# Expert tiles of a two-layer decoder: a counted loop with four places, or straight code with six

## The reference

```python
logits = flat @ router_w.T                      # 2048 tokens, 16 experts
_, topk_idx = jax.lax.top_k(logits + router_bias, 2)
# combine[n, e]: the share of expert e in token n, two non-zero entries a token
for e in range(16):
    h = jax.nn.silu(flat @ Wu[e]) * (flat @ Wg[e])      # 512 -> 256
    out = out + combine[:, e:e + 1] * (h @ Wd[e])       # 256 -> 512
# and one shared expert of twice the width
```

## Time and profile before

| | us |
|---|---|
| median of 3 runs | 2899.99 |
| lowest and highest | 2896.42, 2900.81 |
| the profiled execution's own time | 2895.5 |
| its span, first to last instruction | 2893.8 |

### The profile page before, as it was taken

How to read it: one execution, slowest core, us unless ns; L and a number is a source line. 1 busy time by engine, 2 the same in 40 slices (tenths; PEclk the granted TensorE clock), 3 DMA queues, 4 the chain that set the end, 5 groups by cost and what they waited for, 6 DMA issues and landing times. The chain is left out here.

```text
span 2893.8 us, 34373 instructions
## 1 busy us (share of the span) xinstructions
PE 2060.3 (71%) x12276; PEld 1397.2 (48%) x12308; DVE 1880.0 (65%) x3042; ACT 1168.0 (40%) x2024; POOL 777.1 (27%) x616
## 2 busy tenths in 40 slices
PE   5999995578787848888569999952002688677760
PEld 5777774122222214555357777730002677555540
DVE  3456555467786746999735566547887333688876
ACT  2323222385665634454223232216872112465540
POOL 1212223005969101110012122210000040566654
PEclk7999997598998879999769999987555589999995
DMA  4432231662425020000033332300001100799965
GB/s 138 96 67 60 52 67 45 165 199 80 134 83 147 29 91 0 1 1 1 0 109 67 67 67 45 67 17 0 0 0 45 60 1 0 256 308 303 309 225 166
DMA packets 83672, 258.06 MB, mean 89 GB/s; under 512 B 17312, under 2 KB 18848, under 8 KB 73424
## 3 DMA queue, kind: packets, MB, share of 16 engines
q0 software_dynamic: 29856, 153.33, 17.6%
q1 hardware_dynamic: 52656, 102.62, 12.9%
q10 hardware_dynamic: 1024, 0.26, 0.0%
HBM read 167.51 MB, written 37.79 MB: 71 GB/s over the span
## 5 line engine op out<-in xcount | busy, mean ns | idle before, releaser
L875 DVE TENSOR_REDUCE x_negm<-x_M 128x2 f32<-128x1024 f32 x256 | 309.2, 1223 | 110.5 <-PE x_M L935 110.0
L824 ACT ACTIVATE x_PT<-x_T 128x512 f32<-128x512 f32 x512 | 280.1, 598 | 199.5 <-PE x_T L955 194.2
L317 ACT ACTIVATE L_attn_PT<-L_attn_T 128x512 f32<-128x512 f32 x320 | 175.4, 595 | 360.5 <-PE L_attn_T L519 360.5
L387 DVE TENSOR_REDUCE L_attn_negm<-L_attn_M 128x2 f32<-128x1024 f32 (+1 forms) x192 | 192.0, 1041 | 59.0 <-PE L_attn_M L500 58.5
L224 POOL DMA_DIRECT2D L_attn_QKS<-L_attn_HL x64 | 34.7, 543 | 600.5 <-ACT L_attn_HL L302 566.7
L955 PE MATMUL x_T<-x_QS,x_KS 49*128 49x512 f32 x512 | 141.2, 548 | 62.9 <-ACT x_PT L824 42.6
L517 PE MATMUL L_attn_T<-L_attn_QKS 97*128 97x256 f32 (+3 forms) x512 | 164.8, 384 | 11.7 <-DMA L_attn_QKS<-L_attn_mT 9.4
L1400 PE MATMUL graph_P<-ident,graph_L 128*128 128x128 f32 x64 | 15.7, 428 | 214.8 <-DVE graph_L L1473 209.5
L964 PE MATMUL x_O<-x_PT,x_V 128*32 128x512 f32 x1024 | 156.2, 686 | 7.1 <-issue 7.1
L1421 ACT ACTIVATE graph_seen_a<-graph_SIM,graph_mid 128x512 bf16<-128x512 f32 x200 | 141.4, 708 | 34.3 <-DVE graph_mid L1453 34.3
L955 PEld LDWEIGHTS x_T<-x_QS,x_KS 49*128 49x128 f32 x512 | 52.2, 201 | 210.7 <-ACT x_PT L824 135.1
(11 more groups left out here) (369 smaller groups left out, 5638.2 us busy)
## 6 DMA issues: line engine op xcount, KB each, us to landing
L_attn_QKS<-L_attn_HL SPq DMA_DIRECT2D x192, 128.0 KB, 4.7
L_attn_QKS<-L_attn_HL POOLq DMA_DIRECT2D x192, 128.0 KB, 4.1
moe_y_rows<-slots_YS SPq DMA_DIRECT2D x48, 256.0 KB, 7.8
x_WRAW<-in_w_gateT POOLq DMA_DIRECT2D x8, 1024.0 KB, 7.2
x_QS<-x_xh SPq DMA_DIRECT2D x128, 64.0 KB, 2.3
x_WRAW<-in_w_upT POOLq DMA_DIRECT2D x8, 1024.0 KB, 5.3
x_WRAW<-in_w_downT POOLq DMA_DIRECT2D x8, 1024.0 KB, 6.0
ffn_w<-x_WTER POOLq DMA_DIRECT2D x12, 512.0 KB, 3.2
```

Source lines behind the costliest of these rows:

```text
L317: ac.activation(PT[:, s, bank], T[:, bank], ACT.Exp, scale=SCALE).then_inc(t_free, 1)
L387: last = ve.tensor_reduce(negm[:, g % 2, h0:h0 + nh, i], src, AX.X, ALU.max, negate=True)
L824: ac.activation(PT[:, s // 4, head(s), :], T[(STEPS_S * g + s) % 3][:], ACT.Exp, scale=SCALE).then_inc(t_free, 1)
L875: ve.tensor_reduce(negm[:, g % 2, u // 4:4:2, u % 4], m[:].rearrange("p (r k) -> p r k", r=2), AX.X, ALU.max, negate=True).then_inc(m_free, 1)
```

## The change

`SLOT_TILES` becomes 47. The sum of ceil(c / 128) over 16 experts with 4096 pairs is at most 47. In `run_slots` the counted loops go: each engine's program is written out for all tiles. RAW and XG have six places, YS four, PICK is gone, and the indirect DMAs read their columns from the tables. GpSimd only issues fetches; VectorE makes all the low parts of the weights, the second up piece as one more instruction between HL and XTL. ScalarE in place of VectorE copies Y to YS, two tiles behind, between HH and XTH. TensorE's order is the same, but its first eight products of U wait for `up_hi`, and the last four for `up_lo`.

```diff
-    SLOT_TILES = 2 * NTILE + NE
+    SLOT_TILES = 2 * NTILE + NE - 1
...
-    RING = 4
-    TURNS = SLOT_TILES // RING
+    RING, LAST = 6, SLOT_TILES - 1
...
-        YS = places("YS", RING, D, F32)
-        PICK = places("PICK", RING, 2, U32)
+        YS = places("YS", 4, D, F32)
...
         @block.gpsimd
         def _(pool):
+            for t in range(SLOT_TILES):
+                n = t % RING
+                if t >= RING:
+                    pool.wait_ge(down_lo, t - RING + 1)
+                    pool.wait_ge(up_lo, 2 * (t - RING + 1))
+                pool.indirect_dma_start(out=XG[n], out_offset=None, in_=T["x_rows"],
+                                        in_offset=bass.IndirectOffsetOnAxis(T["slot_token"][:, t:t + 1], 0)
+                                        ).then_inc(x_in[n], 16)
+                pool.indirect_dma_start(out=RAW[n], out_offset=None, in_=weights,
+                                        in_offset=bass.IndirectOffsetOnAxis(T["weight_row"][:, t:t + 1], 0)
+                                        ).then_inc(w_in[n], 16)
...
         @block.scalar
+            def take_y(t):
+                act.wait_ge(y_full, t + 1)
+                if t >= 4:
+                    act.wait_ge(y_out[t % 4], 16 * (t // 4))
+                ac.activation(YS[t % 4], Y[t % 2][:], ACT.Copy).then_inc(y_taken, 1)
+
+            up_weights(0)
+            turned(0)
+            for t in range(SLOT_TILES + 2):
+                if t < LAST:
+                    up_weights(t + 1)
+                if 1 <= t <= SLOT_TILES:
+                    act.wait_ge(ht_full, t)
+                    ac.activation(HH[:], HT[:, 0:F], ACT.Copy).then_inc(h_hi, 1)
+                if t >= 2:
+                    take_y(t - 2)
+                if t < LAST:
+                    turned(t + 1)
+                if t <= LAST:
+                    act.wait_ge(u_full, t + 1)
+                    ac.activation(SU[t % 2], U[t % 2][:, 0:F], ACT.Silu).then_inc(silu_done, 1)
+                    if t >= 2:
+                        act.wait_ge(y_full, t - 1)
+                    ac.activation(WH[t % 2][:, DOWN], RAW[t % RING][:, DOWN], ACT.Copy).then_inc(down_hi, 1)
...
         @block.vector
+            for t in range(SLOT_TILES + 1):
+                if t < LAST:
+                    up_rest(t + 1, 0)
+                if t >= 1:
+                    dve.wait_ge(h_hi, t)
+                    ve.tensor_tensor(HL[:], HT[:, 0:F], HH[:].bitcast(F32), ALU.subtract).then_inc(h_lo, 1)
+                if t < LAST:
+                    up_rest(t + 1, 1)
+                    turned_rest(t + 1)
+                if t <= LAST:
+                    dve.wait_ge(silu_done, t + 1)
+                    ve.tensor_tensor(H[t % 2], SU[t % 2], U[t % 2][:, F:], ALU.mult).then_inc(h_made, 1)
+                    dve.wait_ge(down_hi, t + 1)
+                    ve.tensor_tensor(WL[t % 2][:, DOWN], RAW[t % RING][:, DOWN], WH[t % 2][:, DOWN].bitcast(F32),
+                                     ALU.subtract).then_inc(down_lo, 1)
```

More of the change, by code:

```diff
@@ L1856, in run_slots @@
         block = ctx.enter_context(nc.Block())
[L1858 to L1869, removed]
         @block.gpsimd
         def _(pool):
[L1873 to L1905, removed]
@@ L1927, in up_weights @@
[L1927 to L1930, removed]
-                for part in PARTS:
[L1932 to L1961, removed]
@@ L2012, in _, with turned_rest, up_rest @@
-            run(dve, step)
+            def turned_rest(t):
+                dve.wait_ge(x_hi, t + 1)
+                ve.tensor_tensor(XTL[t % 2], XT[:], XTH[t % 2].bitcast(F32), ALU.subtract).then_inc(x_lo, 1)
+            def up_rest(t, part):
+                dve.wait_ge(up_hi, 2 * t + part + 1)
+                cols = PARTS[part]
+                ve.tensor_tensor(WL[t % 2][:, cols], RAW[t % RING][:, cols], WH[t % 2][:, cols].bitcast(F32),
+                                 ALU.subtract).then_inc(up_lo, 1)
@@ new lines, in turn_tokens @@
+                    last = pe.transpose(XT[:, P * k:P * (k + 1)], XG[t % RING][:, P * k:P * (k + 1)], C["ident"][:])
+                last.then_inc(xt_full, 1)
+            turn_tokens(0)
+            for t in range(SLOT_TILES + 1):
+                i = t % 2
+                if t <= LAST:
+                    ups = [(xp, wp, k) for xp, wp in ((XTH[i], WH[i]), (XTL[i], WH[i]), (XTH[i], WL[i]))
+                           for k in range(KC)]
+                    product = lambda n: pe.matmul(U[i][:], ups[n][0][:, P * ups[n][2]:P * (ups[n][2] + 1)],
+                                                  ups[n][1][:, 2 * F * ups[n][2]:2 * F * (ups[n][2] + 1)],
+                                                  start=(n == 0), stop=(n == len(ups) - 1))
+                    t_.wait_ge(up_hi, 2 * t + 2)
+                    t_.wait_ge(x_lo, t + 1)
+                    if t >= 2:
+                        t_.wait_ge(h_made, t - 1)
+                    for n in range(8):
+                        product(n)
+                if t >= 1:
+                    t_.wait_ge(h_made, t)
+                    if t >= 2:
+                        t_.wait_ge(h_lo, t - 1)
+                    for h in range(2):
+                        last = pe.transpose(HT[:, P * h:P * (h + 1)], H[1 - i][:, P * h:P * (h + 1)], C["ident"][:])
+                    last.then_inc(ht_full, 1)
+                if t <= LAST:
+                    t_.wait_ge(up_lo, 2 * t + 2)
+                    for n in range(8, 12):
+                        last = product(n)
+                    last.then_inc(u_full, 1)
+                if t < LAST:
+                    turn_tokens(t + 1)
+                if t >= 1:
+                    r = 1 - i
+                    t_.wait_ge(h_lo, t)
+                    t_.wait_ge(down_lo, t)
+                    if t >= 3:
+                        t_.wait_ge(y_taken, t - 2)
@@ L2069, in step @@
                             n += 1
-                    last.then_inc(q["y_full"], 1)
-            run(t_, step)
+                    last.then_inc(y_full, 1)
 def combine_slots(nc, X, T):
```

129 lines of the change are left out of this document (27 added, 102 removed).

## The result

| | before | after |
|---|---|---|
| median of 4 runs, side by side | 2899.71 | 2809.12 |
| lowest and highest | 2896.42, 2900.81 | 2806.16, 2816.00 |
| span of the profiled execution | 2893.8 | 2804.4 |
| landing of tile 0 to that of the last | 319.46 in 47 steps | 236.64 in 46 steps |
| period in the steady part | 6.83 | 5.14 |

The ratio on record is 0.9683, with a 95% interval of 0.9654 to 0.9712 (the two medians divided give 0.9688). The forecast of 2826 us was 17 us above the median.

What follows compares the result with a forecast made beforehand. The prediction took a ring of late weight fetches and VectorE's standstill beside GpSimd as the bound, period 6.83 us. Compute bound 5.0 plus 0.3 gave T = 5.35, and 2580.1 + 46 T gave 2826 us, range 2808 to 2856.

Steps and rivals of the forecast that it cites:

- The sign: Whole kernel: faster by more than 6 us at 0.95, within it 0.02, slower 0.03.
- The standstill of VectorE beside GpSimd: Expert stage: VectorE stands still while GpSimd subtracts, which costs VectorE 1.61 us a tile.
- I add 0.3: T = 5.35: Expert stage: 0.3 us added to the new period T for varying landings that rings of two can't fully even out.
- The compute bound of 5.0: Expert stage: the engines' sums and the loops between them allow a period of 5.0 us per tile.
- the tokens' chain: Longest loop between engines: turning 0.60, XTH 0.60, XTL 0.68, U to next turning 2.96, three handovers of about 0.05: 5.0 us.
- the formula: Whole kernel: the time in us is 2580.1 + 46 T, with T the new period of the expert stage.
- rival A: Expert stage: the DMA engines' present busy time stays the bound despite deeper queues, T = 6.2, 2867 us; chance 0.12.
- both bounds of DMA: Fetches and writes of a tile: lower end 4.93 us at 431 and 389 GB/s, upper end 6.2 at 310 GB/s.
- Loops: Unrolling itself: PICK copies ahead of the first fetch go, an estimated 0.4 us once, and semaphore instructions between waits.
- Rival B: Expert stage: mixing reads and writes keeps DMA at 350 to 370 GB/s, T = 5.6 to 6.0, 2838 to 2856 us; chance 0.17.
- Rival C: Expert stage: VectorE's subtractions hold up GpSimd's fetch issues, deciding from 2.5 us per issue, slower than before from 3.2; chance 0.03.
- four sums of 4.7 to 5.1: Expert stage: four resources stand at 4.7 to 5.1 us a tile each, with nothing idle.

Runs made afterwards that it cites:

- e2: The changed kernel with the second up piece subtracted on GpSimd again, six places kept: 2850.62 us, period 6.25.
- e8: The kernel before (loops, four places, 48 tiles, eviction on VectorE) with only all low parts of the weights moved to VectorE: 2904.87 us, period 6.35.
- e1: The changed kernel with four places for RAW and XG in place of six: 2836.85 us, period 5.91.
- e10: e5 with two more swaps: ScalarE makes XTH ahead of the eviction, VectorE makes XTL ahead of the second up piece: 2829.05 us, ratio to before 0.9684.
- e9: The changed kernel run once more, unaltered, on a third chip: 2833.89 us against 2921.53 for before there, ratio 0.9715.
- e4: The kernel before with its counted loops written out and nothing else changed: 2914.81 us, period 6.85.
- e12: The changed kernel with four places and Y evicted by VectorE: 2884.21 us, period 6.16.
- e5: The changed kernel with TensorE turning the next tile's tokens ahead of the last four products of U: 2834.73 us, ratio to before 0.9701.

## Where the prediction was right, and which step of it failed

**The sign and the mechanisms hold.** The standstill of VectorE beside GpSimd is shown by e2, and e8 shows it undone. The late fetches are shown by e1. The eviction took 0.594 where 0.6 was assumed, VectorE is busy 0.956 of the window where near 0.95 was forecast, and the drain, the first landing and the combining stage kept their length within 0.7 us.

**The failed step is "I add 0.3: T = 5.35".** It was an allowance for landings that vary. The row of after that it should have shown in is ScalarE's wait for RAW, and after tile 1 there is none. Six places take the variation up; the two places of WH and WL never see it. The compute bound of 5.0 was itself 0.14 too low: the tokens' chain has the stations and the length of turning, XTH and XTL as worked out, but from U to the next turning it is 3.07 us (2566.27 to 2569.34), not the 2.96 of the earlier trace rows, and the three handovers come to 0.18 in place of 0.15. The traces show where the 0.11 are: nearly all of it in the first four products. Of TensorE's U in the old trace, and of one tile of e10 in the thick of the stage:

```profile
2796.03 0.87 PEld L2033 LDWEIGHTS slots_U<-slots_WH,slots_XTH 128*128 128x128 f32 x4
...
2797.16 1.07 PE L2033 MATMUL slots_U<-slots_WH,slots_XTL 128*128 128x512 f32 x4
```

```profile
2609.91 1.07 PE L1963 MATMUL slots_U<-slots_WH,slots_XTH 128*128 128x512 f32 x4
...
2610.82 1.07 PE L1963 MATMUL slots_U<-slots_WH,slots_XTL 128*128 128x512 f32 x4
```

In the old trace the load of weights starts 0.23 us ahead of its product (2796.03 and 2796.26), under the products of Y, and the second four follow after 0.90. In after the load had waited for XTL, starts 0.03 ahead (2566.24 and 2566.27), and the second four follow after 1.00. e10, where that wait is gone, is back at 0.91 with every engine full. A stretch measured without a stall was too short for a loop in which TensorE stalls once in each turn. So the terms "0.3 for landings" and "5.0" should have been 0 and 5.14. In the profiled spans the forecast of 2820.0 stands 15.6 us above 2804.4: 46 times 0.206 are 9.5 of it, the stages ahead 5.4 (5.8 less the 0.4 expected for PICK), and drain and end 0.7. With 5.14 the formula gives 2817 us; of the 7.6 us that then remain 5.4 are the stages ahead, which the prediction took as fixed and which e9 shows to vary with no change in the kernel, 0.7 drain and end, and 1.5 that the median lies 4.7 us above the profiled span, not 6.2.

**Slips in the working.** At T = 6.2 the formula gives 2865 us for rival A, not 2867. The range doesn't span both bounds of DMA, as it says: 4.93 gives 2807, just below 2808, and 6.2 gives 2865, which it leaves out.

**The fetches** came at the rate of the lower end, but not with four to five of them outstanding. From issue to landing the weights took 9.4 us in the median in before, 10.0 in e1 and 11.5 in after, which is 1.4, 1.7 and 2.2 periods. So some two fetches under way were enough to go from 310 to 423 GB/s; the other places held weights that had landed or were in use.

**Loops.** The forecast gave them 0.4 us once. e4 agrees for before (6.85 against 6.83). It doesn't carry over to the other arrangement: from e8 to e12, with VectorE no longer held up, 0.19 us a tile go with loops and PICK, and the first chain of waits in e8 shows GpSimd waiting for PICK.

**Rival A** (share 0.92 is a full pipe, T = 6.2) is refuted: 411 to 423 GB/s with reads and writes mixed, and 5.24 us of busy time a tile (1.02 of 5.14) where it was 6.28 (0.92 of 6.83). e1 shows why the old row misled: four places alone bring the same kernel from 411 to 423 GB/s down to 351 to 363.

**Rival B** (350 to 370 GB/s when mixed) is refuted by the same windows. The Trainium skill (DMA: Bandwidth & Descriptors, Specifications) gives about 358 GB/s per core, which is the 716 of a stack divided by its two cores. This kernel ran on one core alone, and the windows show 411 to 423 GB/s over 80 us, so that figure was no ceiling here. The reason why mixing would not hurt was only guessed from one-way rows, and held.

**Rival C** (issues held up by VectorE) is there in kind and costs nothing in after: 1.69 and 1.23 us, 2.9 in sum, plus 0.3 of issue, in a period of 5.14. Two issues beside VectorE's subtractions, of after and of e1:

```profile
2564.24 1.22 DVE L1925 TENSOR_TENSOR slots_WL<-slots_RAW,slots_WH 128x1024 fp32r<-128x1024 f32 x1
...
2565.05 1.22 POOL L1866 DMA_INDIRECT slots_RAW<-in_experts,moe_weight_row  x1 [0.30 <-issue]
```

```profile
2600.43 0.94 POOL L1863 DMA_INDIRECT slots_XG<-moe_x_rows,moe_slot_token  x1 [3.06 <-DVE slots_WL L1944]
...
2601.00 1.23 DVE L1925 TENSOR_TENSOR slots_WL<-slots_RAW,slots_WH 128x1024 fp32r<-128x1024 f32 x1 [0.84 <-ACT slots_WH L1885]
```

In after the subtraction is under way when the issue starts, and the issue ends 0.81 us after it (2566.27 against 2565.46). So it is with every issue of after between 2530 and 2700: all 65 end 0.80 to 0.83 us after the subtraction that they met. In e1 the issue starts first and takes its 0.94, and so do the other issues of that kind. The fuller DMA queues are not the cause: e8, at 332 GB/s, has the same 0.80 to 0.83, and e10 and e5 move the same 421 GB/s while the issue of RAW takes 1.97 and 1.51, as in e10 it meets the subtraction earlier. The point of decision, 2.5 us per issue, was out of reach: an issue stands behind one subtraction, not three, which makes 2.0 us at most (1.22 + 0.82, an estimate from these rows; e10 has 2.00). The Trainium skill (SBUF — State Buffer, Who interferes with whom) would leave descriptor writing untouched by such an operation. The traces do not agree, and they decide: the issues waited for it.

**What the forecast missed in weighing** is that the four sums of 4.7 to 5.1 made the order within a step the lever. e5 and e10 get 5.7 and 7.6 us out of the stage by three swaps of independent work, down to where the fetches bound it.

## What to carry to other kernels

When several engines have nearly equal sums, write down the cycle that hands the work round and add an allowance for variation only where a buffer between producer and consumer is too shallow to take it. A busy share of the DMA engines says little by itself: 0.97 was not full (two more places took it from 351 to 363 up to 411 to 423 GB/s), and 1.02 was not the bound (6% fewer bytes gave no time); a run with fewer bytes or more places tells. Compare stages from their own first to last instruction when the stages ahead vary by more than the change is worth.

## What the hardware showed

- One core moved 411 to 423 GB/s with reads and writes mixed, seven eighths of it by indirect DMAs, as much as the 431 of the one-way stretch in the earlier trace rows within 5%.
- The code ahead of the expert stage, the same but for the number of tiles and places, took 2458.9 to 2489.2 us in the six kernels that stand beside a before of 2896 to 2901 us (before, after, e1 to e4), and 2491 to 2501 in the eight on the two other chips. Two things are in it. Among those six the granted clock of the stretch 600 to 1060 goes with it (0.83 in e4 against 0.88 in before). On the two others that clock was 0.85 to 0.88, and the stretch of the shared expert took 171 to 174 us in place of 147 to 150. A single profile can so hide or feign 30 us.
- In the 26 tiles of before between 2520 and 2700, VectorE's subtraction of 128x1024 ended 1.08 to 1.10 us after the end of GpSimd's (2.4 us), whether it had begun 0.57 or 0.81 us into it: it got nearly nothing done beside it. In e2 it is 1.07 to 1.10 us, 28 times. Where VectorE's had begun 0.7 us first (2598.05 above), it kept its 1.22 us and GpSimd's took 2.75 in place of 2.41.
- An issue of an indirect DMA that starts while VectorE subtracts 128x1024 with both inputs in SBUF ends 0.80 to 0.83 us after that subtraction, so it takes up to 2.0 us in place of 0.94 (65 issues in after, 70 in e10). One that starts first keeps its 0.94 to 0.96 (24 in e1, 14 in e2). It had no cost in after, whose GpSimd waits 1.9 us a tile for a place; in e10, where 0.9 us are left, its part isn't told apart from that of the transfers.
